# Delta-rule attention and expert layer on one core: a new order of work on five engines, and the pair rows of A laid out by halves

## The chip, the cores and the metric
One core of a Trainium2 chip runs the whole program. The metric is the device time of one execution in microseconds. The engines are PE (TensorE), DVE (VectorE), ACT (ScalarE), POOL (GpSimd) and SP (SyncE, which only issues transfers here). Each runs its own list of instructions in order; semaphores tie them together.

## The reference, cut to what matters
x is 4 x 2048 x 512 in fp32. First an attention layer: a gated delta rule with 16 heads of 32, then a gated projection, a layer norm and a residual. Its recurrence, for each batch and head:

```python
def step(S, inp):
    k_t, q_t, v_t, beta_t, a_t = inp
    S = S * a_t[..., None, None]
    kv_mem = jnp.einsum('bhd,bhde->bhe', k_t, S)
    delta = (v_t - kv_mem) * beta_t
    S = S + k_t[..., :, None] * delta[..., None, :]
    y_t = jnp.einsum('bhd,bhde->bhe', q_t, S)
    return (S, y_t)
```

Behind it stands an expert layer: each token takes the best of 16 columns (logits from a similarity and a small gate network), 512 to 128 with gelu, back to 512, a layer norm, a residual.

## The kernel before, in words
Two stages. The first walks the 2048 positions in 32 blocks of T = 64 for all four batches at once; the second, the expert stage, sorts tokens by column and runs tiles of 128 rows of one column. The change touches only the first.

A block has two chunks c of C = 32 positions, and each chunk two halves j of CS = 16. G = 16 groups (batch x four heads) lie along the free axis, HP = 4 heads down the 128 partitions, 32 each. Inside a chunk the recurrence is a triangular system: `A` (key products times decays) couples the positions. It is solved by substitution in `solve_half` (L1193 to L1221): for each of 15 positions DVE multiplies row t0 of `pairs` by the solved column of `uk` (L1213, into `Ut`) and subtracts it from the rest (L1216), in two turns of half the groups. Every partition of a head needs every row of A, so `decay_products` (L1187) writes `Ak`, SP writes it to DRAM (`pair_rows`, L303) and `fetch_pairs` reads it back, each row broadcast to 32 partitions (L312); POOL multiplies it by beta (`pairs_times_beta`, L997), then `pr_ready` lets the solve go. `pairs[j]` is one buffer a half, freed by the solve of that half.

The engines run as a software pipeline. In one `step` a block is `chain` (its recurrence), the next one is `ahead` (its projections, norms, decays, keys), the one before is `after` (output projection, residual, gating logits, ranks, scatter). PE, ACT, DVE and POOL unroll two steps into a loop body, `Fori(0, NT // 2 - 1)`; SP's loop has one. The order in each `step` is written out by hand and is an in-order queue: an instruction that waits holds all behind it. PE's wide results go through three PSUM banks `work0` to `work2`; the list TURNS gives the order of their uses, and each use waits until the reader of three uses ago has freed the bank (`into`, L393; all projections are L402).

The chain of one step: `state_to_u` (PE, S times decayed keys, L446, 128 small 32x32 products) gives `uk_full`; DVE's `solve_half(0,0)`; PE's `first_half_to_u` (L456, `corr_full`); `solve_half(0,1)`; PE's `change_state` (L478, `su_full`); DVE's `add_to_state` (L1228, `S_ready`); then the same for chunk 1. `state_to_outputs` (L464) and `chunk_to_outputs` (L469) make outputs beside it. At the end of a step DVE does `choose_columns` (L1273 on: logits, argmax, waits for ACT at L1278 and at L1292), `rows_of_tokens` (L1301 on, waits for PE's `ranks`), and last `add_to_state`.

Of the kernel before, what the change touches and what calls it, by code (L numbers as in the profile page):

```python
# [44 lines left out]
PIECE = CS // 2  # L45
PIECES = [(0, 0), (PIECE, PIECE)]
# [3 lines left out]
    ("xT", 0), ("xT", 1), ("qk", 0), ("rms", 0), ("alpha",), ("qk", 1), ("rms", 1), ("ss", 0),  # L50
    ("wo", 0), ("wo", 1), ("qk", 2), ("ss", 1), ("G", 0), ("G", 1), ("qk", 3),
    ("ss", 2), ("gate", 0), ("ss", 3), ("gate", 1), ("beta", 0), ("xfT", 0), ("xfT", 1), ("beta", 1), ("hid",),
    ("v", 0), ("logits",), ("v", 1), ("rank",)]
# [20 lines left out]
def sandwich_kernel(nc, x, w_in, wa, dt_bias, a_log, norm_w, wo, bo, col_emb, gw1, gb1, gw2, gb2,  # L74
                    w_cols, b_cols, proj_w, proj_b, ln_g, ln_b,
                    c_sq, c_sel, c_mask, c_iota, c_pad, c_tok, c_row, c_col, out, xs_dram):
    with ExitStack() as ctx:
# [57 lines left out]
        Ak = [sb(f"Ak{c}", [P, C, G]) for c in range(NC)]  # L135
# [4 lines left out]
        pairs = [sb(f"pairs{j}", [P, CS, CS, G]) for j in range(2)]  # L140
# [32 lines left out]
        sel_flat = pairs[0][:].rearrange("p s t g -> p (s t g)")  # L173
# [21 lines left out]
        def in_qr(*shape, dt=F32):  # L195
# [40 lines left out]
            pr_ready Ak_ready rows_out kkq_full kkq_free A_ready kt_ready kd_ready kqd_ready  # L236
# [9 lines left out]
        m_xs, m_wc = ([sem(f"{n}{u}") for u in range(MQ)] for n in ("m_xs", "m_wc"))  # L246
        pairs_free, pairs_in = ([sem(f"{n}{j}") for j in range(2)] for n in ("pairs_free", "pairs_in"))
# [19 lines left out]
        pair_rows = nc.dram_tensor("pair_rows", (NC, HP, C, C * G), F32, kind="Internal").ap()  # L267
# [21 lines left out]
        def _(sp):  # L289
# [10 lines left out]
            def fetch_pairs(c):  # L300
                sp.wait_ge(s["Ak_ready"], 1)
                sp.sem_inc(s["Ak_ready"], -1)
                sp.dma_start(pair_rows[c].rearrange("h s r -> (h s) r"), Ak[c][:].rearrange("p t g -> p (t g)")).then_inc(s["rows_out"], 16)  # L303
                sp.wait_ge(s["rows_out"], 16)
                sp.sem_inc(s["rows_out"], -16)
                for j in range(2):
                    sp.wait_ge(pairs_free[j], 1)
                    sp.sem_inc(pairs_free[j], -1)
                    for s0, t0 in PIECES:
                        for h in range(HP):  # L310
                            rows = pair_rows[c, h, j * CS + s0:j * CS + s0 + PIECE, (j * CS + t0) * G:(j + 1) * CS * G]
                            sp.dma_start(pairs[j][DH * h:DH * h + DH, s0:s0 + PIECE, t0:CS, :].rearrange("p s t g -> p s (t g)"),  # L312
                                         rows.unsqueeze(0).to_broadcast([DH, PIECE, (CS - t0) * G])).then_inc(pairs_in[j], 16)
# [16 lines left out]

            load_tokens(0)
            load_tokens(1)
            fetch_pairs(0)
            fetch_pairs(1)
            load_tokens(2)
            fetch_pairs(0)
            with sp.Fori(0, NT - 3) as i:
                load_residual(i)
                fetch_pairs(1)
                load_tokens(i + 3)  # L340
                store(i)
                fetch_pairs(0)
            load_residual(NT - 3)
            fetch_pairs(1)
            load_tokens(NT - 1)
            store(NT - 3)
            fetch_pairs(0)
            load_residual(NT - 2)
            fetch_pairs(1)
            store(NT - 2)  # L350
            load_residual(NT - 1)
            store(NT - 1)
# [36 lines left out]
        def _(pe):  # L389
# [59 lines left out]
            def first_half_to_u(c, half):  # L449

                if not half:
# [5 lines left out]
                    uk[q, g, CS:C], delT[c][q_half, g, :], Ak[c][q_half, CS:C, g],  # L457
# [94 lines left out]
            def step(p, chain, after, ahead):  # L552

                if chain:
                    state_to_u(0, 0)
                    state_to_u(0, 1)
# [54 lines left out]
                if ahead:  # L613
                    decays(1)
# [945 lines left out]
```

## Time and profile before

| | before |
|---|---|
| median of 3 runs | 4272.6 us (4265.62 to 4274.22) |
| profiled execution | 4266.35 us, span 4264.5 us |
| mean granted PE clock | 0.844 of full |
| PE, DVE, POOL, ACT busy | 75%, 67%, 48%, 29% |
| DMA | 388 MB, 91 GB/s mean |

Busy is the time in instructions, not in waits. In rows of instructions, "out<-in partitions x elements xcount | busy us, mean ns | idle us before, by what it ended". A trailing q, as in DVEq, is the engine's own queue of waits: the line named is that of the wait. "issue" is idle time for which the profile shows no wait.

### The profile page before, as it was taken

Reading aid. Unit: us, or ns where it says so; the run is one execution under the profiler, and the core shown is the slowest. Engines: PE = TensorE matmul, PEld = TensorE weight load, DVE = VectorE, ACT = ScalarE, POOL = GpSimd, SP = SyncE. Lnnn points to the kernel's source line nnn. Section 1 sums busy time; section 2 is a strip of 40 time slices with the busy share of each in tenths; the row PEclk is TensorE's granted clock in tenths of the full one; section 3 lists DMA queues with packets and bytes.
Section 4 is the critical chain, followed back from the end, with each engine's and each line's share of the span. In section 5 each row is a group of like instructions: output and inputs, shape, how many; then the busy total and the mean of one; then the engine's idle time right before and its main releaser. Section 6 shows DMA issues by size and latency. Waiting matters only on the chain. (4 is left out here: it accounts for less than half of the span.)

```text
span 4264.5 us, 151843 instructions
## 1 busy us (share of the span) xinstructions
PE 3206.8 (75%) x59364; PEld 2424.2 (57%) x59364; DVE 2863.6 (67%) x12347; ACT 1247.4 (29%) x2119; POOL 2051.5 (48%) x3051
## 2 busy tenths in 40 slices
PE   5787878888788888887888887888887885355553
PEld 4566656666566666666666666666666664233332
DVE  1676767777776767776777676767777776565655
ACT  2233333333333333333333233333333331111110
POOL 1444444444444444444444444444445443277776
PEclk9898888988888989888988898888898896677766
DMA  4444444433344444444434343434444442466663
GB/s 114 77 86 87 86 86 81 84 73 82 75 85 82 86 86 86 87 86 86 86 77 86 79 89 76 86 75 83 84 86 86 86 86 49 140 151 145 150 150 75
DMA packets 416983, 388.41 MB, mean 91 GB/s; under 512 B 42816, under 2 KB 346560, under 8 KB 415824
## 3 DMA queue, kind: packets, MB, share of 16 engines
q1 hardware_dynamic: 399696, 345.37, 38.0%
q0 software_dynamic: 16640, 33.71, 3.8%
q8 instruction: 492, 8.06, 0.8%
q14 instruction: 155, 1.27, 0.1%
HBM read 307.22 MB, written 75.93 MB: 90 GB/s over the span
## 5 line engine op out<-in xcount | busy, mean ns | idle before, releaser
L402 PE MATMUL work<-xT,w_sb 128*128 128x256 f32 x5120 | 1387.6, 421 | 122.9 <-PEq L393 101.8
L997 POOL TENSOR_TENSOR pairs<-pairs,beta 128x240 f32<-128x240 f32 (+14 forms) x1920 | 938.7, 529 | 982.2 <-POOLq L993 982.2
L402 PEld LDWEIGHTS work<-xT,w_sb 128*128 128x128 f32 x5120 | 1029.4, 209 | 337.1 <-issue 186.1
L1213 DVE TENSOR_TENSOR Ut<-pairs,uk 128x120 f32<-128x120 f32 (+14 forms) x3840 | 833.3, 255 | 25.6 <-DVEq L1204 20.9
L1216 DVE TENSOR_TENSOR uk<-uk,Ut 128x120 f32<-128x120 f32 (+14 forms) x3840 | 708.2, 226 | 0.0
L446 PE MATMUL uk<-kqd,S 32*32 32x32 f32 x8192 | 121.4, 216 | 243.5 <-PEq L445 186.5
L510 PE MATMUL work<-wo_sb,ctxT 128*128 128x512 f32 x512 | 269.6, 687 | 17.2 <-PEq L393 17.2
L1200 DVE TENSOR_TENSOR uk<-vT,uk 128x128 f32<-128x128 f32 x256 | 63.3, 293 | 311.2 <-DVEq L1320 186.2
L986 POOL TENSOR_TENSOR kqd<-kq,eg 128x1024 f32<-128x1024 f32 x64 | 150.5, 2352 | 231.4 <-POOLq L1053 231.4
L446 PEld LDWEIGHTS uk<-kqd,S 32*32 32x32 f32 x8192 | 106.5, 127 | 272.9 <-issue 272.4
L771 ACT ACTIVATE qraw<-work 128x512 f32<-128x512 f32 x128 | 75.9, 593 | 628.2 <-ACTq L770 628.2
L728 PE MATMUL kkq<-w_sb,kq 128*128 128x512 f32 x160 | 130.6, 913 | 104.3 <-PEq L727 104.3
L1034 POOL TENSOR_TENSOR x<-x,y 128x512 f32<-128x512 f32 x64 | 81.3, 1270 | 247.8 <-POOLq L1033 247.8
L510 PEld LDWEIGHTS work<-wo_sb,ctxT 128*128 128x128 f32 x512 | 110.9, 223 | 153.7 <-issue 152.5
L708 PE MATMUL work<-squares,w_sb 128*128 128x128 f32 x320 | 70.2, 367 | 166.7 <-PEq L706 166.4
L708 PEld LDWEIGHTS work<-squares,w_sb 128*128 128x128 f32 x320 | 51.7, 191 | 213.5 <-issue 213.3
L436 PEld LDWEIGHTS kkq<-kq 32*32 32x32 f32 x8192 | 135.3, 115 | 57.5 <-issue 57.5
L464 PE MATMUL uq<-kqd,S 32*32 32x32 f32 x8192 | 102.4, 200 | 83.5 <-issue 83.5
L1135 POOL DMA_INDIRECT out<-pairs,qr x80 | 130.0, 1624 | 72.3 <-POOL pairs L1133 33.7
L956 ACT ACTIVATE kq<-work 128x512 f32<-128x512 f32 x80 | 47.8, 597 | 387.4 <-ACTq L954 387.4
L436 PE MATMUL kkq<-kq 32*32 32x64 f32 x8192 | 156.9, 230 | 4.1 <-issue 4.1
L456 PEld LDWEIGHTS uk<-Ak,delT 16*32 16x32 f32 x8192 | 88.7, 113 | 117.8 <-issue 117.8
(190 smaller groups left out, 5637.7 us busy)
## 6 DMA issues: line engine op xcount, KB each, us to landing
pairs<-pair_rows SPq DMA_DIRECT2D x512, 256.0 KB, 5.0
pairs<-pair_rows SPq DMA_DIRECT2D x512, 128.0 KB, 6.3
w_sb<-xs_rows SPq DMA_DIRECT2D x80, 258.0 KB, 2.8
w_sb<-in_w_cols SPq DMA_DIRECT2D x80, 256.0 KB, 4.1
w_sb<-in_proj_w SPq DMA_DIRECT2D x80, 256.0 KB, 4.3
xt<-in_x SPq DMA_DIRECT2D x66, 256.0 KB, 3.8
pair_rows<-Ak SPq DMA_DIRECT2D x64, 256.0 KB, 2.0
x<-in_x SPq DMA_DIRECT2D x64, 256.0 KB
```

The costliest lines, as they stand in the source:

```text
L402: mm = pe.matmul(w[:, half * BT:(half + 1) * BT], w_sb[:, f, j * D + hg * P:j * D + (hg + 1) * P], xT[:, f, :], start=(f == 0), stop=(f == ...
L436: on_tiles(half, "kkq_full", lambda g, q, q_half: pe.matmul(kkq[q, g], kq[q, g, c, 0, :], kq[q, g, c].rearrange("p a t -> p (a t)"), start ...
L446: on_tiles(half, "uk_full", lambda g, q, q_half: pe.matmul(uk[q, g], S[q, g, :], kqd[c][q, g, 0, :], start=(g == 0), stop=True, skip_group ...
L464: on_tiles(half, None, lambda g, q, q_half: pe.matmul(uq[q, g], S[q, g, :], kqd[c][q, g, 1, :], start=(g == 0), stop=True, skip_group_chec ...
L510: mm = pe.matmul(w, flat(ctxT[:, hg * B + tb * BL:hg * B + (tb + 1) * BL, :]), wo_sb[:, hg, :], start=(hg == 0), stop=(hg == KD - 1))
L708: mm = pe.transpose(m_tp[u % 2][:, f * P:(f + 1) * P], xs[u][:, f * P:(f + 1) * P], ident)
L728: pe.matmul(m_yp[u % 2], hm[u % 2], pw[u], start=True, stop=True).then_inc(s["m_y"], 1)
L986: link(nc.gpsimd.tensor_tensor(kqd[c][:], kq[:, :, c], eg[:, :, c * C:(c + 1) * C].unsqueeze(2).to_broadcast([P, G, 2, C]), ALU.mult))
L997: ins = nc.gpsimd.tensor_tensor(a, a, beta[:, :, t:t + WID[t0]].rearrange("p g t -> p t g"), ALU.mult)
L1135: nc.gpsimd.indirect_dma_start(out_rows, bass.IndirectOffsetOnAxis(ap=toki[:, u:u + 1].bitcast(U32), axis=0), z[u], None, bounds_check=ROW ...
L1213: link(v.tensor_tensor(Ut[:, g, 0:n], pr[:, g], uk[:, g, at:at + 1].to_broadcast([P, G // 2, n]), ALU.mult), behind=1)
L1216: link(v.tensor_tensor(uk[:, g, at + 1:at + 1 + n], uk[:, g, at + 1:at + 1 + n], Ut[:, g, 0:n], ALU.subtract), behind=1)
```

## The change
SP: the transfer of A by way of DRAM is split in `write_rows` and `fetch_pairs(c, j)`. `pairs` and `Ak` change places of position and group, so that positions of one half are adjacent, and `pair_rows` has one part for each half. A half is fetched in four transfers, one a head, of one run of 15 rows for each partition, in place of eight, in which the part left of the diagonal block was left out.

```diff
-            def fetch_pairs(c):
+            def write_rows(c):
                 sp.wait_ge(s["Ak_ready"], 1)
                 sp.sem_inc(s["Ak_ready"], -1)
-                sp.dma_start(pair_rows[c].rearrange("h s r -> (h s) r"), Ak[c][:].rearrange("p t g -> p (t g)")).then_inc(s["rows_out"], 16)
-                sp.wait_ge(s["rows_out"], 16)
-                sp.sem_inc(s["rows_out"], -16)
-                for j in range(2):
-                    sp.wait_ge(pairs_free[j], 1)
-                    sp.sem_inc(pairs_free[j], -1)
-                    for s0, t0 in PIECES:
-                        for h in range(HP):
-                            rows = pair_rows[c, h, j * CS + s0:j * CS + s0 + PIECE, (j * CS + t0) * G:(j + 1) * CS * G]
...
+                sp.dma_start(pair_rows[c].rearrange("j h s n -> (h s) j n"), Ak[c][:].rearrange("p j g t -> p j (g t)"))\
+                    .then_inc(rows_out[c], 16)
+            def fetch_pairs(c, j):
+                if not j:
+                    sp.wait_ge(rows_out[c], 16)
+                    sp.sem_inc(rows_out[c], -16)
+                sp.wait_ge(pairs_free[j], 1)
+                sp.sem_inc(pairs_free[j], -1)
+                for h in range(HP):
+                    rows = pair_rows[c, j, h, j * CS:j * CS + CS - 1, :].rearrange("s n -> (s n)")
+                    sp.dma_start(pairs[j][DH * h:DH * h + DH, 0:CS - 1].rearrange("p s g t -> p (s g t)"),
+                                 rows.unsqueeze(0).to_broadcast([DH, (CS - 1) * G * CS])).then_inc(pairs_in[j], 16)
...
+            def step(chain, after, ahead, block, following):
+                if chain:
+                    fetch_pairs(0, 1)
+                if after:
+                    load_residual(block)
+                if chain:
+                    write_rows(1)
+                    fetch_pairs(1, 0)
+                    fetch_pairs(1, 1)
+                if ahead:
+                    load_tokens(following)
+                    write_rows(0)
+                    fetch_pairs(0, 0)
+                if after:
+                    store(block)
...
-        Ak = [sb(f"Ak{c}", [P, C, G]) for c in range(NC)]
+        Ak = [sb(f"Ak{c}", [P, 2, G, CS]) for c in range(NC)]
-        pairs = [sb(f"pairs{j}", [P, CS, CS, G]) for j in range(2)]
+        pairs = [sb(f"pairs{j}", [P, CS, G, CS]) for j in range(2)]
...
-                    uk[q, g, CS:C], delT[c][q_half, g, :], Ak[c][q_half, CS:C, g],
+                    uk[q, g, CS:C], delT[c][q_half, g, :], Ak[c][q_half, 1, g, :],
...
-                    a = pairs[j][:, t0, t0 + 1:CS, :]
+                    a = pairs[j][:, t0, :, t0 + 1:CS]
...
-                    ins = nc.gpsimd.tensor_tensor(a, a, beta[:, :, t:t + WID[t0]].rearrange("p g t -> p t g"), ALU.mult)
+                    ins = nc.gpsimd.tensor_tensor(a, a, beta[:, :, t:t + WID[t0]], ALU.mult)
...
-                    pr = pairs[j][:, t0, t0 + 1:CS, :].rearrange("p t g -> p g t")
+                    pr = pairs[j][:, t0, :, t0 + 1:CS]
```

SP's order was load_residual, fetch_pairs(1), load_tokens, store, fetch_pairs(0), the last with both of its halves.

The order in the other four engines, of a step that has all three roles (TURNS is changed to match). Numbers in brackets are (chunk, half), or the part.

PE after: u(0,0), chunk_to_outputs(1,0), u(0,1), xT(0), chunk_to_outputs(1,1), xT(1), key_products(1,0) (1,1), qk0, log_alpha(0) (1), output squares (0) (1), first half of qk1, squares 0, first_half_to_u(0,0) (0,1), second half of qk1, output_projection(0), state_to_outputs(0,0), qk2, output_projection(1), state_to_outputs(0,1), squares 1, decays(0) (1), change_state(0,0) (0,1), qk3, u(1,0) (1,1), squares 2, gate 0 first half, chunk_to_outputs(0,0), squares 3, chunk_to_outputs(0,1), gate 0 second half, gate 1 first half, first_half_to_u(1,0) (1,1), gate 1 second half, state_to_outputs(1,0), key_products(0,0), state_to_outputs(1,1), beta 0 first half, key_products(0,1), beta 0 second half, xfT(0), beta 1, xfT(1), gate_hidden, change_state(1,0), v 0, gate_logits(0), change_state(1,1), gate_logits(1), v 1, ranks. Before, both halves of output_projection stood together, state_to_outputs(0) stood right behind first_half_to_u(0), state_to_outputs(1) between the halves of beta 1, chunk_to_outputs(1,0) behind u(0,1) and xT(0), and change_state(1,0) and (1,1) behind v 1's first half and behind ranks.

DVE, the hand-written list (the end of it in full):

```diff
                     solve_half(0, 0)
+                if ahead:
+                    alpha_argument()
+                if chain:
+                    decay_products(1)
+                if after:
+                    normed_outputs(0)
+                if ahead:
+                    log_alpha()
...
                     solve_half(1, 0)
+                if ahead:
+                    scale(2)
+                    scale(3)
...
+                    link(v.tensor_tensor(flat(unit(silu[1 - p], 0)), bank("gate", 0), sg[:], ALU.mult))
...
+                    dve.wait_ge(s["dec_ready"], 2)
+                    dve.sem_inc(s["dec_ready"], -2)
+                    decay_products(0)
...
+                    link(v.tensor_tensor(flat(unit(silu[1 - p], 1)), bank("gate", 1), sg[:], ALU.mult))
...
                     solve_half(1, 1)
-                if ahead:
-                    dve.wait_ge(s["dec_ready"], 2)
-                    dve.sem_inc(s["dec_ready"], -2)
-                    decay_products(0)
-                    next_tokens_norm()
...
                     rsqrt(rstd[:], ve[:], nt1[:])
+                if ahead:
+                    next_tokens_norm()
+                if after:
+                    logits_of_columns()
+                if chain:
+                    add_to_state()
+                if after:
                     choose_columns()
+                    weigh_columns()
                     rows_of_tokens()
-                if chain:
-                    add_to_state()
```

Between solve_half(0,1) and solve_half(1,0) DVE now has y's first half, scale(0), y's second half, token_norm, add_to_state, scale(1), the two transposes of G; before, scale(0), both halves of y, token_norm, scale(1), add_to_state, the transposes. x1's statistics stand behind silu 0 instead of ahead of scale(2). The key transposes stand behind log_alpha instead of right behind solve_half(0,0).

POOL: the gating of ctxT and the copy of la stand ahead of the kd products instead of behind them; decay_state(1) right behind pairs_times_beta(1,0), ahead of the first difference of G; the residual sum between the two differences. ACT: the exponentials for alpha between the two inverse_rms; copy_outputs(0) behind pair_decays(1), both inverse_norms and the sigmoid of gate 0; the sigmoid of gate 1 ahead of the norm of x1; xfT(0)'s copy ahead of beta 0.

## Rows read from the trace of the kernel before

**Rows 1.** DVE, line L1228 (add_to_state): one row of the timeline, and the source view.
```profile
187.95 0.69 DVE L1228 TENSOR_TENSOR S<-Sd,su 128x512 f32<-128x512 f32 x1 [0.37 <-DVEq L1227]
L1228 DVE TENSOR_TENSOR S<-Sd,su x64: 686/687/689, 145.9 to 3603.0; 128x512 f32<-128x512 f32 x64
```

**Rows 2.** Windows, first stage: us, then PE, PEld, DVE, ACT, POOL busy, clock, DMA.
```profile
188.64:3554.36 3365.72, 2742.38 (x55388) 2098.69 (x55388) 2385.21 (x11105) 1095.62 (x1838) 1570.77 (x2361) 0.87 0.41 84
```

**Rows 3.** Waits of DVE from 200 to 3580 us: total, times, longest.
```profile
DVE uk L1200 <- DVEq L1320: 179.0, 30, 8.8
DVE lt L1273 <- DVEq L1271: 90.3, 30, 5.0
DVE uk L1200 <- DVEq L1362: 75.2, 31, 4.9
DVE l L1293 <- DVEq L1292: 73.2, 30, 3.9
DVE kq L1237 <- DVEq L1236: 70.2, 120, 2.4
DVE silu L1376 <- DVEq L1375: 57.8, 60, 1.9
DVE S L1228 <- DVEq L1227: 52.9, 61, 3.1
```

**Rows 4.** Waits of PE in the same stretch.
```profile
PE work L402 <- PEq L393: 96.3, 31, 4.4
PE uq L464 <- issue: 80.3, 31, 4.1
```

**Rows 5.** Timeline of DVE at the end of one step: start, us, instruction, idle before.
```profile
1621.44 0.19 DVE L1273 TENSOR_TENSOR lt<-work,gb_sb 128x32 f32<-128x32 f32 x1 [2.22 <-DVEq L1271]
1631.36 0.69 DVE L1228 TENSOR_TENSOR S<-Sd,su 128x512 f32<-128x512 f32 x1 [0.37 <-DVEq L1227]
1636.50 0.49 DVE L1200 TENSOR_TENSOR uk<-vT,uk 128x128 f32<-128x128 f32 x2 [4.46 <-DVEq L1320]
```

**Rows 6.** Timeline of PE: a turn of the loop, mid-step, a step's end without turn.
```profile
1515.34 0.75 PE L478 MATMUL su<-delT,kd 32*32 32x32 f32 x64
1522.79 0.54 PE L446 MATMUL uk<-kqd,S 32*32 32x32 f32 x22 [6.70 <-PEq L445]
1553.79 0.86 PE L464 MATMUL uq<-kqd,S 32*32 32x32 f32 x49 [3.53 <-issue]
1626.46 0.78 PE L478 MATMUL su<-delT,kd 32*32 32x32 f32 x64
1632.25 1.68 PE L446 MATMUL uk<-kqd,S 32*32 32x32 f32 x92 [5.01 <-PEq L445]
1635.61 0.74 PE L446 MATMUL uk<-kqd,S 32*32 32x32 f32 x36 [1.68 <-issue]
```

**Rows 7.** Windows with the granted clock (third number from the end).
```profile
1553.00:1557.00 4.00, 3.21 (x52) 1.90 (x52) 4.00 (x25) 0.00 (x0) 2.13 (x3) 0.50 0.05 11
1571.00:1590.00 19.00, 16.12 (x432) 12.54 (x432) 14.87 (x72) 11.06 (x19) 15.88 (x22) 1.00 0.20 58
```

**Rows 8.** DVE by line over the whole run (the first two from the page).
```profile
L1213 DVE TENSOR_TENSOR Ut<-pairs,uk 128x120 f32<-128x120 f32 (+14 forms) x3840 | 833.3, 255 | 25.6 <-DVEq L1204 20.9
L1216 DVE TENSOR_TENSOR uk<-uk,Ut 128x120 f32<-128x120 f32 (+14 forms) x3840 | 708.2, 226 | 0.0
...
L1187 DVE TENSOR_TENSOR Ak<-kkq,dec 128x512 f32<-128x512 f32 x64 | 66.1, 1033 | 24.2 <-DVEq L1185 24.2
L1189 DVE TENSOR_TENSOR Aq<-kkq,dec 128x512 f32<-128x512 f32 x64 | 44.2, 691 | 9.4
```

**Rows 9.** POOL by line and shape.
```profile
L997 POOL TENSOR_TENSOR pairs<-pairs,beta 128x240 f32<-128x240 f32 x128 | 104.5, 816 | 982.2 <-POOLq L993 982.2
...
L1012 POOL TENSOR_TENSOR kd<-kd,dec 128x512 f32<-128x512 f32 x62 | 66.7, 1076 | 99.2 <-POOLq L1010 93.6 <-POOL kd L1012 5.5
```

**Rows 10.** Windows while pairs are fetched: DMA share and GB/s stand last.
```profile
1545.00:1553.00 8.00, 5.26 (x218) 3.79 (x218) 5.33 (x21) 4.07 (x8) 3.49 (x3) 0.97 1.05 196
```

More of the change, by code:

```diff
@@ L44 @@
 NW = 3
-PIECE = CS // 2
-PIECES = [(0, 0), (PIECE, PIECE)]
+PAIRS_IN = 16 * HP
 TURNS = [
[L50 to L53, printed above, removed]
+    ("xT", 0), ("xT", 1), ("qk", 0), ("alpha",), ("rms", 0), ("rms", 1), ("qk", 1), ("ss", 0), ("wo", 0),
+    ("qk", 2), ("wo", 1), ("ss", 1), ("G", 0), ("G", 1), ("qk", 3), ("ss", 2), ("gate", 0), ("ss", 3),
+    ("gate", 1), ("beta", 0), ("xfT", 0), ("beta", 1), ("xfT", 1), ("hid",), ("v", 0), ("logits",), ("v", 1),
+    ("rank",),
+]
 BANK = {use: n % NW for n, use in enumerate(TURNS)}
@@ L602, in step @@
                     output_projection(0)
-                    output_projection(1)
+                if chain:
+                    state_to_outputs(0, 0)
                 if ahead:
@@ L606, in step @@
                     project("qk", 1, 0, 1)
+                if after:
+                    output_projection(1)
+                if chain:
+                    state_to_outputs(0, 1)
+                if ahead:
                     squares_sum(1)
@@ L638, in step @@
                 if chain:
-                    first_half_to_u(1, 1)
+                    state_to_outputs(1, 0)
                 if ahead:
-                    project("beta", 3, 0, 0)
                     pe.wait_ge(s["kq_ready_pe"], 4)
@@ L645, in step @@
                     key_products(0, 0)
+                if chain:
+                    state_to_outputs(1, 1)
+                if ahead:
+                    project("beta", 3, 0, 0)
+                    key_products(0, 1)
                     project("beta", 3, 0, 1)
-                    key_products(0, 1)
                 if after:
@@ L674, in step @@
                     project("v", 2, 1, 0)
-                if chain:
-                    change_state(1, 0)
-                if ahead:
                     project("v", 2, 1, 1)
@@ L1321, in step @@
                     solve_half(0, 0)
+                if ahead:
+                    alpha_argument()
+                if chain:
+                    decay_products(1)
+                if after:
+                    normed_outputs(0)
+                if ahead:
+                    log_alpha()
+                if chain:
                     for c in range(NC):
@@ L1336, in step @@
                     solve_half(0, 1)
+                if after:
+                    dve.wait_ge(s["wo_full"], 1)
+                    dve.sem_inc(s["wo_full"], -1)
+                    link(v.tensor_tensor(y[:, 0, :], bank("wo", 0), bo_sb[:], ALU.add))
+                    dve.sem_inc(bank_free("wo", 0), 1)
+                    token_stats(y, 0)
                 if ahead:
```

245 lines of the change are left out of this document (111 added, 134 removed).

## The prediction, made before the changed kernel ran

> **What bounds the kernel now.** First the period. The last S update of a step (second add_to_state) stands at 187.95 in the second step and at 3603.0 in the last with 31 periods between [rows 1], so a step takes 110.2 us. That stage is four fifths of the span; the expert stage behind it is not touched. Then the shares: in it PE is busy 2742 of 3366 us and DVE 2385 [rows 2]. Neither is full, so the next view is what each waits for. DVE's 24 rows of waits between 200 and 3580 us add up to 846 us over 30.7 steps, 27.6 us a step; seven carry it [rows 3]. The largest, 179 us, is the first solve of a step waiting for state_to_u. PE waits for DVE at the same place (uk), for a bank of work that DVE or ACT frees (96 us), and in "issue" rows for nothing that the profile shows: 80 us in the row shown, 226 in all seven, 7.4 a step [rows 4]. So no engine binds; the step is a chain handed between DVE and PE, and its two hand-overs at the step's end are the dearest. There DVE has the logits at 1621.44 but updates S only at 1631.36, behind choosing and ranking, and then idles 4.46 us until uk is there [rows 5]. PE has finished at 1627.2 and can't start u before 1632.25. At a turn of the loop (every second step) it is worse: PE's last work starts at 1515.34 and ends at 1516.1, S is ready at 1519.15, u starts at 1522.79 and stops once more [rows 6]. The PE clock pays too: 0.50 of full (the 1.2 GHz level) at 1553 to 1557, after the stop of 3.53 us ahead of L464 [rows 6], but 1.00 (2.4 GHz) at 1571 to 1590, ahead of which it had hardly stopped [rows 7].
>
> **Layout of Ak and pairs.** DVE's L1213 reads pairs with t 16 elements apart: 833.3 us for 3840, against 708.2 for the 3840 of L1216, of the same shapes, which read runs. L1187, which writes Ak 16 apart, takes 1033 ns against 691 for L1189 with the same operands in runs [rows 8]. So runs are worth up to 125 us / 128 solves = 0.98 us a solve, 3.9 a step, and 2 x 0.34 for L1187: 4.6 us a step. Bounds: 0 (if L1213 is slow for its broadcast second operand) and 4.6; I take 4.6, since L1187 pays for the stride with no broadcast. The Trainium skill ("SBUF — State Buffer", Door 1) has 16-byte lines, so that fp32 four apart is free and sixteen is not; by that the broadcast is innocent. PE's moving operand in first_half_to_u turns from strided to runs too; products of this kind take no more now than those of runs do, so nothing.
> POOL's L997 (816 ns at 240 elements [rows 9]) gets runs of n instead of 16 and a beta read in runs. No row shows short runs. L1012, in runs of 32 with a broadcast operand, costs 1076 ns for 512, 2.1 ns an element against 3.4 here: between 2 us cheaper and some 7 us dearer (double) than the 7.2 of a half. I take no change; the half is hidden behind a solve or more while it stays under about 10 us (below).
>
> **Transfers.** A half now sends 128 x 15 KB, 1.97 MB instead of 1.57, in 4 issues instead of 8. In 1545 to 1553 the queue is full at 196 GB/s [rows 10]. At that rate a half takes 10.0 us instead of 8.0; if long runs went at twice the rate, 5. I take 10. It is hidden either way: pairs for (1,0) are asked for at about 17 us of the step and used past 40, (1,1) from 31 to 66, (0,0) from about 66 to 90, (0,1) from 77 to 106, less POOL's 7.2 each. Ak leaves in 1 KB runs instead of 2 KB: 0 to 1 us, hidden too. SP's order changes: load_tokens now stands ahead of write_rows(0) and waits for xt_free (ACT's copies of G, some 20 us before Ak exists), and store, with its wait for landing, stands behind fetch (0,0) and ahead of fetch (0,1), which waits for the solve's end anyway. No cost. The Trainium skill ("SBUF — State Buffer", Door 1) has a rule that speaks against this part: 32 partitions reach only 8 of 16 ports, about 218 GB/s, however long the run. The row's 196 agrees; by it a half takes 9.0 us, by a rule of run length alone 5, and the sum stays.
>
> **The tail of the step.** add_to_state goes ahead of choose, weigh and rows, and change_state ahead of the last projections. DVE then does about 6 us (2.0 choose, 1.2 weigh, 1.8 rows, gaps) while PE makes ranks and u. But ranks still waits for choose, and PE is in order: after oh_ready it needs 1.2 for ranks, then u half 0.7, the moved chunk_to_outputs 0.84, u half 0.7, and the fetch stop of 1.7 that stands in u now [rows 6]: uk at +5.2. DVE is through at +4.4, of which 1.4 is the wait for e. Together 2.1 us of wait instead of 4.3 + 2.4: 4.6 gained in a step without a turn. With a turn PE loses its 6.7 us from its last work to u [rows 6] wholly behind ranks; uk comes at +12 to 13 and DVE waits about 10 instead of 10.6: 0.6 gained. Mean 2.6. POOL: slot, its two scatters and the wait for them now stand ahead of decay_state and kqd by some 9 us after S; Sd is wanted 50 us later, pairs (0,1) end at about 19 us of the step and are used at 21. That cover is the thinnest of all, 2 to 3 us.
>
> **The middle.** I walked the new order once with the durations of rows at full clock. DVE's wait for the uk of chunk 1 falls from 2.4 to 0.6. output_projection 1 behind qk2, wo0 freed earlier: scale and S waits fall by 1.0 and 0.6. silu0 stands ahead of x1's statistics, freeing the gate bank 5 us sooner: silu waits down 1.1, and PE's 96 us of bank waits shrink. alpha, outputs, corr, gT: down 0.8, 0.5, 0.6, 0.3. The added wait: decay_products(0) now stands ahead of solve (1,1) and waits for key_products(0), about 1.4 us, with silu1 and the solve queued behind it and change_state behind them; the wait for logits falls as much, as less DVE work lies behind the solve. state_to_outputs(0) is spread between projections, which gives its instruction fetch time: the 2.6 us stop there (80.3 us over the stage [rows 4]) goes, but PE has slack there in part, so it is in the waits above.
>
> **Sum.** DVE's step: 110.2 - 27.6 = 82.6 of work and gaps; less 4.6 layout = 78.0; waits 27.6 - 2.6 - 1.8 - 1.0 - 0.6 - 1.1 - 0.8 - 0.5 - 0.6 - 0.3 = 18.3. Period 96.3. PE's side stands just under it: its work at full clock is about 83 us a step, plus 4 us of waits, 3.3 of fetch stops and 7/2 for the turn, 94. But the same walk made of the order of before gives 104.8, 5.4 under the 110.2 that ran, for cold clock and short stops. With fewer long stops I keep 4 of these 5.4 (bounds 0 and 5.4): 100.3. So 9.9 x 31 = 307 us off 4264.5, which is 3958; the execution has 1.85 us around its span: 3960. The median of the runs, 4272.6, stands 6.3 above the profiled execution, inside their scatter; I leave it.
>
> **Rivals.**
> A. PE loses nothing: 96.3 a step, 431 us less, 3835. For: the long stops go. Against: the turn's stays, and 128 more 32x32 products stand in one burst at the step's head.
> B. The stride is not what L1213 pays: DVE 3.9 a step longer, of which PE's waits swallow a third: 102.9, 4040.
> C. PE keeps all that it loses and binds: it is busy 82% of the stage now, the turn is uncovered, and u, outputs and keys now make one burst of 384 small products, two stops of 1.7 where there was one. Then only the layout counts: 105.6, 143 us less, 4123.
> D. POOL's short runs cost double, 14.4 a half: pairs (0,1) end 4 to 5 us after solve (0,1) could start: 105, 4105. It decides from 10 us a half.
> E. Slower: PE's instruction fetch shares the 16 engines with the pairs traffic, full 8 to 10 us for each of four halves a step [rows 10]. Packets of 15 KB instead of 1 KB could hold each block of instructions back; three blocks held 5 us each are 15 us against the 9.9 gained: 115.3, 4424. It decides from 3.3 us a block. For: the stop of 3.53 us ahead of L464 lies beside such traffic [rows 6]. Against: blocks arrive during it today. The Trainium skill ("Runtime: NRT & Kernel Launch", Instruction fetch mechanics) calls the crossing of a block mostly hidden and a taken branch a stall; by it E and half of C are out. The trace says otherwise of the crossing (226 us) and agrees on the branch.
> F. The gains cancel with a wait I don't see (a bank held over a turn of DVE): no change, 4266.
>
> **How the numbers follow.** Forecast (3890 to 4040 of its own) 0.48, A 0.10, B 0.12, C 0.15, D 0.05, E 0.07, F 0.03. Faster by over 0.2% (about what a measurement of this kernel tells from no change): 0.90; within 0.03; slower 0.07. Range 3865 to 4130: it leaves out E, F, most of A and the forecast's edges, 0.2 in all.
>
> **What would show it.** L1213's mean of 255 ns down to L1216's 226 and L1187 near 691 (else B); L997 at 240 elements near 816 (else D); the first solve's wait small in every second step and about 8 us at turns; logits to S update under 2 us instead of 9.9; PE "issue" rows for L464 near zero (above 15 us a step in all: E); granted clock of the stage above 0.87 (at 0.87 with PE over 90% busy: C). The sum is wrong most easily in the 4 us of losses and in waits that replace others in the middle.

## The result, and the profile after

The changed kernel takes 4104.6 us (median of 4 runs, 4095.9 to 4109.1) against 4273.4 before: a ratio of 0.9606, 95% interval 0.9586 to 0.9626, 169 us less. 3960 was forecast, with a range up to 4130. The direction and the range hold; little more than half of the forecast gain came, and the forecast's own band had ended at 4040. The profiled execution has a span of 4102.2 us and a mean clock of 0.874.

The period first, as in [rows 1]: the source view of add_to_state's S update, which now is L1222.

```profile
L1222 DVE TENSOR_TENSOR S<-Sd,su x64: 686/687/689, 141.1 to 3431.5; 128x512 f32<-128x512 f32 x64
```

The S update at the end of the second step, in the timeline:

```profile
186.93 0.69 DVE L1222 TENSOR_TENSOR S<-Sd,su 128x512 f32<-128x512 f32 x1 [0.85 <-DVEq L1221]
```

So the period is (3431.5 - 186.9) / 31 = 104.66 us, 5.5 less than before. 31 periods give 170.5 us, and the stage is the whole result. (Behind the last S the run is 9 us longer than before, 670.7 us against 661.5, about what S now stands earlier in its step.) The stage's window, answering to [rows 2]:

```profile
186.93:3431.54 3244.61, 2662.14 (x56092) 2059.57 (x56090) 2383.25 (x11266) 1101.58 (x1855) 1502.75 (x2364) 0.91 0.44 102
```

DVE is as busy as before, 2383 us, although its layout saving is in there. The lines by engine, answering to [rows 8] and [rows 9]; the last two are of one and the same operation, before and after:

```profile
L1210 DVE TENSOR_TENSOR uk<-uk,Ut 128x120 f32<-128x120 f32 (+14 forms) x3840 | 709.9, 227 | 0.0
L1207 DVE TENSOR_TENSOR Ut<-pairs,uk 128x120 f32<-128x120 f32 (+14 forms) x3840 | 690.2, 216 | 6.0 <-DVEq L1198 1.3
L1179 DVE TENSOR_TENSOR Ak<-kkq,dec 128x512 f32<-128x512 f32 x64 | 44.2, 691 | 136.0 <-DVEq L1177 136.0
...
L986 POOL TENSOR_TENSOR pairs<-pairs,beta 128x240 f32<-128x240 f32 x128 | 89.4, 699 | 791.7 <-POOLq L982 791.7
```
```profile
L1237 DVE TENSOR_TENSOR kq<-qraw,qr 128x512 f32<-128x512 f32 x128 | 93.3, 729 | 90.0 <-DVEq L1236 90.0
```
```profile
L1231 DVE TENSOR_TENSOR kq<-qraw,qr 128x512 f32<-128x512 f32 x128 | 133.2, 1041 | 62.1 <-DVEq L1230 61.6 <-ACT qr L780 0.5
```

The solve's products fell from 255 to 216 ns and Ak from 1033 to 691. Operations that read SBUF only rose: the scaling of q and k from 729 to 1041 ns. Then the waits of DVE and of PE from 200 to 3400 us, answering to [rows 3] and [rows 4]:

```profile
DVE uk L1194 <- DVEq L1316: 161.8, 30, 10.9
DVE Ak L1179 <- DVEq L1177: 126.3, 61, 6.9
DVE S L1222 <- DVEq L1221: 88.6, 61, 5.4
...
DVE uk L1194 <- DVEq L1368: 36.9, 31, 6.2
...
DVE l L1289 <- DVEq L1288: 12.2, 30, 3.4
```
```profile
PE uk L452 <- issue: 69.3, 36, 3.7
PE work L516 <- PEq L399: 63.5, 24, 7.0
...
PE su L484 <- issue: 49.1, 15, 4.4
PE work L408 <- PEq L399: 44.4, 57, 1.4
...
PE uq L470 <- issue: 34.5, 22, 2.5
```

The wait for logits (90 us before) is 8.8, choose's second wait is down to 12.2, and a row of 126.3 us stands for decay_products, where the kernel before had 18. PE's stop ahead of state_to_outputs fell from 80.3 us to 34.5, but others came: all "issue" rows add up to 7.8 us a step, against 7.3.

The end of a step without a turn, and the first solve behind a turn, answering to [rows 5] and [rows 6]:

```profile
1541.08 0.19 DVE L1267 TENSOR_TENSOR lt<-work,gb_sb 128x32 f32<-128x32 f32 x1 [0.79 <-DVEq L1265]
...
1541.98 0.69 DVE L1222 TENSOR_TENSOR S<-Sd,su 128x512 f32<-128x512 f32 x1 [0.37 <-DVEq L1221]
...
1549.41 0.49 DVE L1194 TENSOR_TENSOR uk<-vT,uk 128x128 f32<-128x128 f32 x2 [0.86 <-DVEq L1316]
```
```profile
1451.78 0.49 DVE L1194 TENSOR_TENSOR uk<-vT,uk 128x128 f32<-128x128 f32 x2 [10.43 <-DVEq L1316]
```

S follows the logits after 0.9 us and not 9.9; the first solve's wait is 0.5 to 2.3 us between turns and 8.8 to 10.9 at each turn.

### The profile page after: what moved, and what is told of

The parts are those of the page before. It is cut to its first block and busy times, and to the rows that moved or that the text cites. A ratio compares the mean times of both kernels' runs of the same rounds, so it can differ in the third digit from the quotient of the medians.

```text
span 4102.2 us, 151331 instructions
## 1 busy us (share of the span) xinstructions
PE 3108.5 (76%) x59364; PEld 2363.5 (58%) x59364; DVE 2832.5 (69%) x12347; ACT 1242.5 (30%) x2119; POOL 1976.1 (48%) x3051
## 3 DMA queue, kind: packets, MB, share of 16 engines
q1 hardware_dynamic: 153936, 395.67, 40.8%
q14 instruction: 155, 1.27, 0.1%
## 5 line engine op out<-in xcount | busy, mean ns | idle before, releaser
L408 PE MATMUL work<-xT,w_sb 128*128 128x256 f32 x5120 | 1299.2, 405 | 66.4 <-PEq L399 51.6
L986 POOL TENSOR_TENSOR pairs<-pairs,beta 128x240 f32<-128x240 f32 (+14 forms) x1920 | 865.0, 488 | 791.7 <-POOLq L982 791.7
L408 PEld LDWEIGHTS work<-xT,w_sb 128*128 128x128 f32 x5120 | 990.5, 200 | 268.4 <-issue 127.0
L1210 DVE TENSOR_TENSOR uk<-uk,Ut 128x120 f32<-128x120 f32 (+14 forms) x3840 | 709.9, 227 | 0.0
L1207 DVE TENSOR_TENSOR Ut<-pairs,uk 128x120 f32<-128x120 f32 (+14 forms) x3840 | 690.2, 216 | 6.0 <-DVEq L1198 1.3
L1055 POOL DMA_INDIRECT xs_rows<-xfw,slot x64 | 63.9, 999 | 369.5 <-POOLq L1053 359.7
L970 POOL TENSOR_TENSOR Sd<-S,eg_end 128x512 f32<-128x512 f32 x64 | 67.5, 1055 | 322.0 <-POOLq L969 318.6
L1000 POOL TENSOR_TENSOR ctxT<-ctxT,silu 128x512 f32<-128x512 f32 x64 | 81.1, 1267 | 255.1 <-POOLq L999 155.8
L484 PE MATMUL su<-delT,kd 32*32 32x32 f32 x8192 | 94.9, 196 | 112.6 <-PEq L483 63.5
L1231 DVE TENSOR_TENSOR kq<-qraw,qr 128x512 f32<-128x512 f32 x128 | 133.2, 1041 | 62.1 <-DVEq L1230 61.6
L442 PEld LDWEIGHTS kkq<-kq 32*32 32x32 f32 x8192 | 151.3, 124 | 36.2 <-issue 34.5
```

Source lines behind the costliest of these rows:

```text
L408: mm = pe.matmul(w[:, half * BT:(half + 1) * BT], w_sb[:, f, j * D + hg * P:j * D + (hg + 1) * P], xT[:, f, :], start=(f == 0), stop=(f == ...
L442: on_tiles(half, "kkq_full", lambda g, q, q_half: pe.matmul(kkq[q, g], kq[q, g, c, 0, :], kq[q, g, c].rearrange("p a t -> p (a t)"), start ...
L484: on_tiles(half, "su_full", lambda g, q, q_half: pe.matmul(su[q, g, :], kd[c][q, g, :], delT[c][q, g, :], start=True, stop=True))
L986: ins = nc.gpsimd.tensor_tensor(a, a, beta[:, :, t:t + WID[t0]], ALU.mult)
L1000: nc.gpsimd.tensor_tensor(unit(ctxT, hp), unit(ctxT, hp), unit(silu[1 - p], hp), ALU.mult)\
L1207: link(v.tensor_tensor(Ut[:, g, 0:n], pr[:, g], uk[:, g, at:at + 1].to_broadcast([P, G // 2, n]), ALU.mult), behind=1)
```

## The experiments

Read them by one sum for each kernel, per step: period = DVE's waits + DVE's work. The waits are all rows of that view over 29 of the 31 periods, divided by 29; the work is the rest. PE's "issue" rows are taken over the same stretch. Ratios are to the kernel before, run beside each. The changed kernel gave 0.9606 and, on another occasion, 0.9645: between groups of runs, differences under 0.4% say nothing. The periods come from one profiled execution of each kernel, on different occasions, and the 110.16 of before serves them all, though its median beside them went from 4268 to 4293 us (0.6%, or 0.8 us a step). Where a period difference matters, the ratio stands beside it, turned into us a step.

| kernel | ratio [95%] | period | DVE work | DVE waits | PE issue stops |
|---|---|---|---|---|---|
| before | 1 | 110.16 | 82.5 | 27.6 | 7.3 |
| e1 layout only | 1.0067 [1.0042, 1.0092] | 111.68 | 77.3 | 34.4 | 10.1 |
| e2 order only | 0.9756 [0.9720, 0.9791] | 107.13 | 86.7 | 20.4 | 7.1 |
| after | 0.9606 [0.9586, 0.9626] | 104.66 | 81.2 | 23.5 | 7.8 |
| e0 after, again | 0.9645 [0.9626, 0.9664] | 105.01 | 81.1 | 23.9 | 7.4 |
| e3 eight transfers | 0.9533 [0.9500, 0.9570] | 104.66 | 81.4 | 23.2 | 7.3 |
| e4 loop of six | 0.9528 [0.9502, 0.9554] | 104.07 | 81.2 | 22.9 | 7.7 |
| e5 one product of 15 | 0.9637 [0.9621, 0.9653] | 104.76 | 77.4 | 27.3 | 7.4 |
| e6 old order, 1 KB | 1.0115 [1.0082, 1.0148] | 112.07 | 77.2 | 34.9 | 10.5 |
| e8 new order, 1 KB | 0.9784 [0.9768, 0.9800] | 106.76 | 80.5 | 26.3 | 7.8 |
| e9 old order, 8 transfers | 0.9972 [0.9952, 0.9992] | 109.47 | 77.0 | 32.4 | 8.2 |
| e10 old order, 12 rows | 0.9825 [0.9786, 0.9865] | 107.69 | 77.1 | 30.6 | 8.3 |
| e7 key products together | 0.9453 [0.9421, 0.9485] | 102.57 | 81.1 | 21.5 | 8.5 |
| e11 together | 0.9235 [0.9208, 0.9261] | 99.87 | 81.1 | 18.8 | 7.6 |

**The two parts apart.** e1 is the old order with the new layout and its four transfers; e2 the new order with the old layout and transfers.

```diff
 # e1: the kernel before, with
+        Ak = [sb(f"Ak{c}", [P, 2, G, CS]) for c in range(NC)]
+        pairs = [sb(f"pairs{j}", [P, CS, G, CS]) for j in range(2)]
...
 # e2: the changed kernel, with
+        Ak = [sb(f"Ak{c}", [P, C, G]) for c in range(NC)]
+        pairs = [sb(f"pairs{j}", [P, CS, CS, G]) for j in range(2)]
...
```

> The order of work of before, with the new layout of Ak, pairs and pair_rows and the four long transfers a half. Theory one (DVE carries the chain, so what DVE saves in L1213 and L1187, 4.6 to 5.3 us a step, comes out of the step nearly whole): 130 to 165 us less than before, about 4120. Theory two (PE holds the step, DVE's saving turns into waiting): under 60 us less, 4215 or more. L1213's mean falls from 255 to about 216 ns under both.

> The new order of work in all five engines, with the old layout and the eight short transfers a half. Theory one (layout and order add up, and the order is worth little because its gain at the loop's turns and beside POOL is lost): the changed kernel plus 140 to 165, so 4245 to 4270, hardly faster than before. Theory two (the order carries the gain, PE binds in it and the layout adds little on top): 4105 to 4150.

Of e1's theories the second is nearer (4215 or more), but neither has room for a kernel that is slower than before; e2's 4181 us lies between its two. The layout takes 5.2 us of DVE's work from a step in the old order and 5.5 in the new, a little over the forecast 4.6. But in the old order the waits grow by 6.8 and the kernel becomes 0.7% slower; in the new one by 3.1, and 2.5 us of period are left. Those 3.1 are spread over the waits for PE: over 29 periods the first solve's goes from 128.8 to 158.8 us, decay_products' from 106.8 to 122.5, S's from 71.7 to 86.9. The order alone gives 3.0: it takes 7.2 of waits away and adds 4.2 of work to DVE. By the ratios the layout costs 0.9 us a step in the old order and gives 1.5 to 2.1 in the new, and the order gives 3.4: the same picture with smaller steps for the layout. PE's waits in e1, to set beside [rows 4]:

```profile
PE uq L462 <- issue: 165.8, 29, 6.8
```

PE stood 2.6 us a step at state_to_outputs(0,0) before (80.3 us in 31 steps); here it is 5.7 (165.8 us in 29). Its place, and the windows around it:

```profile
1574.10 0.86 PE L462 MATMUL uq<-kqd,S 32*32 32x32 f32 x79
1581.11 0.86 PE L462 MATMUL uq<-kqd,S 32*32 32x32 f32 x49 [6.14 <-issue]
```
```profile
1570.00:1572.00 2.00, 2.00 (x69) 1.19 (x68) 0.90 (x2) 1.58 (x4) 0.00 (x0) 1.00 0.94 207
1572.00:1574.00 2.00, 2.00 (x66) 1.54 (x66) 0.99 (x3) 1.10 (x3) 0.22 (x1) 1.00 1.04 238
1574.00:1576.00 2.00, 0.96 (x107) 0.87 (x96) 1.59 (x8) 1.38 (x3) 2.00 (x2) 1.00 1.06 223
1576.00:1578.00 2.00, 0.00 (x0) 0.00 (x0) 2.00 (x13) 0.00 (x0) 1.27 (x2) 0.84 0.76 154
1578.00:1580.00 2.00, 0.00 (x0) 0.00 (x0) 2.00 (x15) 0.00 (x0) 0.00 (x0) 0.50 0.27 58
```

PE stops in the middle of 128 products of one kind, with no wait on it, while a fetched half moves (DMA share about 1), and goes on when that has drained. The clock falls to 0.50 meanwhile. What it stops for is in the DMA queues. The page lists one named "instruction", here with 492 packets of 16384 bytes. The queues in e1 from 1575 to 1578, from 1578 to 1580 and over the whole run:

```profile
q1 hardware_dynamic: 50, 0.52, 86.0%
```
```profile
q1 hardware_dynamic: 22, 0.09, 20.9%
q8 instruction: 1, 0.02, 4.2%
```
```profile
q8 instruction: 492, 8.06, 0.8%
```

In the first 3 us of the stop only data moves. The one instruction packet starts at 1578.4, when the half has drained, and lands at 1579.7; PE goes on at 1581.1, 1.4 us later. It is so everywhere: between 200 and 3400 us PE has 70 "issue" stops of 1 us or more in e1, 78 in the kernel before and 94 in the changed one, and each of them ends 1.2 to 1.8 us after such a packet has landed. In e1 the stop also stands at the same product each time, behind the 79th of the 128 in one kind of step and behind the 22nd in the other (28 of 29 rows). So PE is short of its next block of instructions, and the blocks come over the same 16 engines as the data. That the data holds them back is one part only: of the 94 stops of the changed kernel, 33 have no packet of data (512 bytes or more) on the engines in the 2 us ahead of the block's own, and they last 1.9 us in the mean and 2.5 at most; the other 61 reach 4.4, and e1's 70, all with data ahead of the block, 3.6 in the mean and 6.8 at most. Three runs asked what about the transfers does it: the length of packets, how fast they are queued, or the bytes.

**Packet length.** A gap behind each row keeps transfers from merging rows: 1024 bytes a packet, 15360 in e1, for the same bytes. (The kernel before sent packets of 1024 and 512 bytes.)

```diff
+ROW_PITCH = G * CS + 64
-        pair_rows = nc.dram_tensor("pair_rows", (NC, 2, HP, C, G * CS), F32, kind="Internal").ap()
+        pair_rows = nc.dram_tensor("pair_rows", (NC, 2, HP, C, ROW_PITCH), F32, kind="Internal").ap()[:, :, :, :, 0:G * CS]
```

> The old order with the new layout (as e1), but with a gap of 256 bytes behind each row of 1 KB in DRAM, so that the transfers can't merge rows: packets of 1024 bytes for the same payload, still four transfers. Theory, the long packets hold back PE's instruction blocks in the old order: the idle time of state_to_outputs put down to issue falls from 5.7 us a step in e1 to about the 2.6 of the kernel before, all issue stops from 10.4 to 7.5, and the time falls by 90 to 150 us under e1, to a ratio of 0.970 to 0.985 against the kernel before. Rival, the loss in e1 is of timing (the pairs land earlier or later than before) and not of packet length: the stops stay over 9.5 us a step and the time stays within 20 us of e1 (ratio 1.002 to 1.012). Second rival, short rows of 1 KB without the old triangular cut take more DMA time than before: slower than e1.

```profile
PE uq L463 <- issue: 144.4, 29, 6.4
```

5.0 us a step and all stops 10.5: the theory of long packets falls. e6 is no faster than e1 either.

**Queueing and bytes.** e9 issues the half as eight transfers, e10 keeps four and leaves three rows out (sizes in these expectations are in KB of 1024 bytes: 1920 KB a half, 1536 before).

```diff
 # e9
+PIECES = [(0, CS // 2), (CS // 2, CS - 1)]
...
-                    for h in range(HP):
+                    for s0, s1 in PIECES:
+                        for h in range(HP):
...
 # e10
+ROWS_IN = 12
...
-                        rows = pair_rows[c, j, h, j * CS:j * CS + CS - 1, :].rearrange("s n -> (s n)")
+                        rows = pair_rows[c, j, h, j * CS:j * CS + ROWS_IN, :].rearrange("s n -> (s n)")
...
```

> The old order with the new layout (as e1), but each half fetched with eight transfers (four of 8 rows, then four of 7) and not four: the same 1.92 MB per half, spread by SP's issuing over 3.7 us and not 1.7. In e1 the stop of PE ahead of state_to_outputs(0,0) ends when the burst has moved: 5.8 to 6.8 us in one kind of step, 4.1 to 6.5 in the other, where the kernel before has 3.5 to 4.1 and 0.9 to 1.2. Theory Q, what counts is how much is queued when PE wants its next block: with eight transfers the second kind of step comes back to 1 to 2 us, the first stays at 5.5 to 6.5; stop per step about 3.7 instead of 5.7, time 40 to 80 us under e1 (ratio 0.988 to 0.997). Theory M, only the bytes of the burst count: both kinds stay as in e1, time within 20 us of it (1.002 to 1.012).

> The old order with the new layout, four transfers, but only 12 of a half's 15 rows fetched: 1.54 MB per half as in the kernel before. The products and the solve of the last three rows read other rows instead, so that part of the computation is left out; the number and shape of all operations stand. Theory M (bytes of the burst): the burst is 0.38 MB shorter, at about 205 GB/s 1.9 us, so the stops fall from 6.1 and 4.9 us to about 4.2 and 3; 3.6 per step, time 40 to 80 us under e1 (ratio 0.988 to 0.997). Theory Q (how much is queued early) gives the first kind of step 4.2 and the second 3 too, since all four are queued at once; so this run and the one with eight transfers together say how the 3.1 us a step are shared. A third reading, the stop has nothing to do with these transfers: unchanged, time within 20 us of e1.

```profile
1552.45 0.86 PE L464 MATMUL uq<-kqd,S 32*32 32x32 f32 x49 [4.85 <-issue]
...
1657.48 1.70 PE L464 MATMUL uq<-kqd,S 32*32 32x32 f32 x106 [2.69 <-issue]
PE uq L464 <- issue: 118.8, 29, 6.0
```
```profile
PE uq L467 <- issue: 126.4, 29, 6.2
1624.09 1.70 PE L467 MATMUL uq<-kqd,S 32*32 32x32 f32 x106 [4.31 <-issue]
```

The first fence is e9, the two kinds of step and the sum over 29 periods; there stops are 4 to 6 us in the one kind and 2.1 to 4.4 in the other, 4.1 a step. In e10 they are mostly 3 to 6 in both, 4.4 a step. So each lever takes some 1.3 to 1.6 of e1's 3.1 extra; neither alone brings the old 2.6 back, and theories M and Q both hold in part. The time follows: 41 us under e1 by the ratio for e9, 103 for e10, which is more than either theory gave it. e10 gives more than its shorter stop: its first solve also waits 1.7 us less a step (161.6 us over 29 periods in place of 211.1). Fewer bytes are fetched for that solve too; how its part divides stays open. With the stop shortened the layout gains in the old order too: 109.47 and 107.69 us a step lie under the 110.16 of before, 111.68 above it.

**The same in the new order.** e3 splits each half in eight; e8 has the gap behind rows.

> The changed kernel, each half of the pairs fetched in eight transfers of 1 KB runs instead of four of 15 KB runs, same bytes, same layout. Theory one (the fetch is hidden and runs don't matter): within 10 us of the changed kernel, 4095 to 4115. Theory two (long packets hold back PE's blocks of instructions): 30 to 100 us faster than the changed kernel. Theory three (long runs shorten a fetch on which something waits): 20 us slower or more.

In e3 rows that lie side by side were merged, so its packets were of 7168 and 8192 bytes and not of 1 KB: it tests the number of transfers, not the packet. Its period is that of after to the digit; whether its ratio is a gain can't be said.

> The changed kernel with the same gap behind each row: packets of 1024 bytes, four transfers. Theory, the new order issues these transfers where PE's stops are already hidden: issue stops a step from 7.8 to 6.5 or 7, time 10 to 40 us under the changed kernel. If the long packets cost as much here as in the old order: 90 us or more under it. Rival, the short packets use more of the queues' time and the pairs come late for the solve: the wait for the products (now nothing) shows up and the time rises by over 20 us.

e8 is slower than e0 beside it, 4174 against 4116 us. Here the page's queue rows, after and e8:

```profile
q1 hardware_dynamic: 153936, 395.67, 40.8%
```
```profile
q1 hardware_dynamic: 383312, 395.67, 46.1%
```

The same 395.67 MB take 5 points more of the engines in short packets. The first solve behind a turn starts about 15.0 us after oh, the input of the ranks, and not 13.4, and that wait and those for Ak and S are where the time went. So in the new order the long packets are no cost but worth 1.4%. In the old order the same step is 0.5%, hardly more than the scatter; why it is less there is open.

**The control.**

> The changed kernel as it is, beside the next three on the same chip, so that each of them has it as a neighbour. Expected: the ratio of its first measurement, 0.9606 within 0.003.

0.9645, just outside.

**DVE beside POOL.** e5 takes away 14 of the 15 products that POOL makes for a half.

```diff
-                for t0 in range(CS - 1):
+                for t0 in range(CS - 2, CS - 1):
                     a = pairs[j][:, t0, :, t0 + 1:CS]
```

> The changed kernel with POOL's products of pairs and beta cut from 15 per half to one, so that part of the computation is left out (the solve reads products that were not multiplied by beta); waits, transfers and all other work stand. Theory: VectorE's operations that read SBUF beside these products are held up (the changed kernel spends 4.38 us a step on the four kq<-qraw,qr against 2.97 before, 1.67 against 0.41 on alog, 1.30 against 0.51 on ve, 2.1 more on the nt and rstd chain). Without the products kq falls to about 0.72 us each, the nt operations to 0.16, ve and alog to under 0.5 a step: 5 to 6 us of VectorE's time a step, 3.5 to 5.5 us off the period of 104.66, a time 110 to 170 us under the changed kernel. Rival, the held-up operations lie beside waits for PE that would take their place: VectorE's busy time falls as said but its waits grow by as much, and the time falls by under 40 us.

```profile
L986 POOL TENSOR_TENSOR pairs<-pairs,beta 128x16 f32<-128x16 f32 x122 | 30.2, 247 | 798.3 <-POOLq L982 790.0 <-POOLq L1044 8.2
```
```profile
DVE Ak L1179 <- DVEq L1177: 146.0, 61, 7.1
DVE lt L1267 <- DVEq L1265: 55.9, 30, 3.2
```

POOL loses 791 us of work, DVE's 2-element operations go back from 224 to 161 ns (L1152) and from 425 to 169 (L1162), the scaling only from 1049 to 915: in both kernels 31 of its 128 stand beside another POOL operation, decay_state's product (L970, 1.06 us), and take 1.58 us, where those beside nothing take 0.69. DVE's work falls by 3.7 us a step, where 5 to 6 were expected, and its waits rise by 3.4: for the logits from 12.1 to 55.9 us, for Ak from 124.8 to 146.0. The time stands, 4109 against 4116. The rival holds: the 3.7 us of slowed work that e5 gives back cost nothing in this order.

**The added wait.** PE's second key product moves up behind the first, ahead of 2.75 us of other work.

```diff
                     key_products(0, 0)
+                    key_products(0, 1)
                 if chain:
                     state_to_outputs(1, 1)
                 if ahead:
                     project("beta", 3, 0, 0)
-                    key_products(0, 1)
```

> The changed kernel with PE's key_products(0, 1) moved up directly behind key_products(0, 0), ahead of state_to_outputs(1, 1) and project beta(0, 0), 2.75 us of PE's work. VectorE's added wait for decay_products(0), 3.75 us in the step looked at, falls to about 1.0, and Ak's waits from 126 us to about 50. Theory, the added wait is on the path: 1.5 to 2.7 us a step, 45 to 85 us under the changed kernel (ratio 0.941 to 0.950). Rival, PE's own work sets the pace by now, so that VectorE waits longer elsewhere (first uk, S, the logits), as with POOL's products cut: within 20 us of the changed kernel (0.957 to 0.967).

```profile
DVE Ak L1179 <- DVEq L1177: 29.8, 61, 1.5
```

126 us of waits become 30, 3.1 a step; the period falls by 2.1 to 2.4, the time by 1.5 to 1.9% of the kernel before. The added wait was on the path, with two thirds to three quarters of its length.

**The turn of the loop.** e4 unrolls six steps instead of two, so that 10 of 15 turns go; the edit is the same in PE, ACT and POOL.

```diff
-            with dve.Fori(0, NT // 2 - 1):
-                step(1, True, True, True)
-                step(0, True, True, True)
+            with dve.Fori(0, (NT // 2 - 1) // UNROLL):
+                for _ in range(UNROLL):
+                    step(1, True, True, True)
+                    step(0, True, True, True)
```

> The changed kernel with six steps instead of two in the loop body of PE, ACT, DVE and POOL, so 5 turns instead of 15. Theory one (a turn costs the step about 8.5 us, the wait of 10.4 us at a turn less the 1.3 us elsewhere, and nothing gives it back later): 60 to 90 us less than the changed kernel, about 4030. Theory two (work held up at a turn is made good within the step, as PE waits less later): under 30 us less, 4075 or more.

```profile
1451.34 0.49 DVE L1198 TENSOR_TENSOR uk<-vT,uk 128x128 f32<-128x128 f32 x2 [10.99 <-DVEq L1320]
...
1659.20 0.49 DVE L1198 TENSOR_TENSOR uk<-vT,uk 128x128 f32<-128x128 f32 x2 [3.67 <-DVEq L1320]
```

The first row is a turn that stayed, the second a place where one was. There the wait is 3.3 to 4.2 us and not 10, 6 less; but in the other steps it rose from 1.2 to 3.0 in the mean, so that the sum fell by 32 us (161.8 to 130.1) and the period by 0.6 to 0.9. By the period that is 18 to 29 us, theory two; by the ratio 33 to 50, between the two.

**Together.** e7, e3 and e4 in one kernel, which beats both.

> The changed kernel with three edits at once: the key products together (ratio 0.9453 alone), a loop of six steps (0.9528 alone) and eight transfers per half (0.9533 alone, but with the changed kernel's own period of 104.66). If the gains add (68 us from the first by period and time, 17 to 35 from the second, 0 to 30 from the third): 3950 to 4020 us, ratio 0.926 to 0.942, period 101.3 to 102.0. If PE's own work and stops set the pace once the wait for the key products is gone, the other two give nothing: ratio 0.943 to 0.947, period 102.4 to 102.7.

```profile
DVE uk L1200 <- DVEq L1322: 100.2, 30, 11.0
```

3959 us (3951 to 3975) against 4290 before beside it, 7.65% less. From e7 to here the period falls by 2.7, more than the two edits gave alone; 1.8 of it is the first solve's wait (153.5 to 100.2), which is back at 0.47 us in 8 of the 15 steps where no turn ever stood, as it was in 10 of them in e7. Which of the two edits does it was not separated.

## Why the prediction was right or wrong

**The frame** was right: the period times 31 is the whole result, the expert stage did not move. That the range holds is owed to rivals C and D, whose times it took in. In the terms of the sum, DVE's work came to 81.2 us a step where 78.0 was forecast, and the waits to 23.5 where 18.3 and 4 of losses were: 3.2 and 1.2, together the 4.4 us by which 100.3 missed 104.66. The experiments divide the same 4.4 otherwise, and say what counted.

**The layout, 4.6 a step.** As a saving of DVE it was right (5.2 and 5.5 measured), and rival B is out: 216 ns lies under the 227 of L1210. The step that failed is taking the whole of it off the period. The text itself read the step as a chain handed between two engines, and then subtracted one engine's work in full. Measured, the layout is worth 2.5 of period in the new order and minus 1.5 in the old. That is 2.1 of the 4.4 us.

**The transfers** were taken as hidden. As data they are: L1207's row has 1.3 us of waits for them in the whole run. As traffic they are not, see E below. Nor was 218 GB/s a ceiling for the four transfers of a half together: e1 moved 238 from 1572 to 1574.

**The order, 5.3 a step (110.2 - 4.6 - 100.3).** Measured 3.0 (e2), the other 2.3. The term at fault is the added wait: 1.4 us forecast, 3.9 measured in the mean (2.4 to 7.0), with key_products(0,1) standing behind two other pieces of PE's work. The text named what is queued behind that wait and set the logits' wait against it, but its walk had the key products ready sooner than they were, and e7 gave 2.1 to 2.4 for moving them. The S waits rose too, 52.9 to 88.6 us, 1.2 a step where a fall of 0.6 was forecast; alpha's rose by 0.4 where a fall of 0.8 was, and those for y, of which the text has nothing, by 0.7. No run takes these apart. The waits for scale, silu and corr fell as forecast, to 0.1 us. The 4 us of losses rested on fewer long stops; PE's "issue" stops went from 7.3 to 7.8 a step.

**The tail.** Right in its size: the waits for uk and for e, [rows 3] 179.0 + 73.2, became 161.8 + 12.2 us, 2.5 a step less against 2.6 forecast, and 10 us at the turns as walked. The logits' wait fell by more than forecast, 90 to 9 us.

**DVE's work.** Not foreseen: the order adds 4.2 us a step, in operations that now stand beside POOL's. That is about the size of the miss, and without e5 it would have passed for its cause; e5 took 3.7 of work away and the time stood.

**The rivals.** D gave the time to the microsecond (4105), and that is luck: its mechanism is out, as L986 takes 699 ns at 240 elements and not 816 or double. C's 105.6 is near too, and half of its reason is true: PE's stops did not fall. The other half is false: it said that only the layout counts, and the order alone gave 3.0 of 5.5. E, slower through PE's blocks held back, had 0.07. Its mechanism is there, but by what is queued and its bytes and not by the packets' length that it named, and its size in the new order is 0.3 to 0.7 us a step of stops (7.1 in e2). In the old order all stops grow by 2.8, beside which the layout alone is slower: of a change without the new order E would have had the sign, though not the size. The Trainium skill ("Runtime: NRT & Kernel Launch", Instruction fetch mechanics) calls the crossing of a block mostly hidden. By count the trace agrees: from 200 to 3400 us 468 instruction packets start in the changed kernel, and 94 of them end a stop of 1 us or more. By cost it doesn't: the stops take 7 to 10.5 us of a step in every kernel here. A (PE loses nothing) and F are out by the time.

**The signs named ahead.** L1207, L1179, the logits and the clock (0.91) came as said. PE's stop at state_to_outputs more than halved where it was to vanish, and the sum of stops did not fall; they moved to u, change_state and first_half_to_u.

## What to carry to other kernels

Before a saving on one engine is taken off a chain, ask who it hands over to: here 3.7 to 5.5 us a step of the same engine's work were worth 2.5, nothing, or less than nothing, and a wait of 3.1 on the hand-over was worth 2.1 to 2.4. For an added wait, walk the producer's queue up to the producer, not only the consumer's. Data fetched by DMA can hold back an engine's instructions: look in narrow windows of the DMA view for the instruction queue's packet ahead of the end of an "issue" stop. Where it comes only as a burst ends, move the burst, split it or make it smaller, and measure a change of layout together with its transfers.

## What the runs showed of the hardware

- PE stopped up to 6.8 us without a wait beside a transfer of 1.97 MB; 1 KB packets changed it little (5.7 and 5.0 us a step), eight transfers for four gave 4.1, a fifth of the bytes less 4.4.
- Each "issue" stop of 1 us or more ended 1.2 to 1.8 us after a packet of 16384 bytes of the instruction queue had landed (78 stops before, 94 after, 70 in e1). Without data ahead of the packet such stops were 1.9 us in the mean (33 of the 94).
- Rows adjacent in DRAM and in SBUF were merged: in e3, 8 and 7 rows of 1 KB, written as separate rows, went as packets of 8192 and 7168 bytes; with a gap behind each row (e6, e8) as 1024.
- DVE operations with all operands in SBUF took longer beside POOL's: in the mean of all, 2-element ones went from 161 to 224 ns (L1152), 512-element ones from 729 to 1041. The Trainium skill ("SBUF — State Buffer", SBUF: two separate sides) calls it a lock on a shared pair of ports, held for a whole instruction. The trace agrees so far as the 0.16 us operations that touch an L986 took 0.48 in the median and 0.71 at most, a scaling beside decay_state's 1.06 us took 1.58 in place of 0.69, and the 32-element L1250 beside POOL's gating of 1.27 us took 1.29 in place of 0.19.
